# A convolution block and a selective scan on one core: the step is kept in PSUM and multiplied there by VectorE, and per-image work is given one SBUF operand or moved to ScalarE

## What is computed

```python
# layer 0: y = depthwise conv of x with per-image weights agg_w
g  = gelu(conv1x1(y, b1)) * conv1x1(y, b2)
x1 = x + layer_norm_over_channels(g)
# layer 1, on tokens of x1
xh, z = split(x1 @ W_in);  xh = silu(causal_conv_k2(xh))
dt_low, B, C = split(xh @ W_x)
dt = softplus(dt_low @ W_dt + b_dt)                    # the step, 256 channels
h  = exp(dt * A) * h + (dt * xh) * B                   # scan over pixels, 16 states a channel
y  = (sum over states of h * C + xh * D) * silu(z)
m  = y @ W_out
out = silu(group_norm(m) * gamma + beta) + x1          # statistics over a whole image
```

## Time and profile before

| what | value |
|---|---|
| median of 3 runs | 15738.19 us (15737.39 to 15739.81) |
| the profiled execution's own time | 15743.65 us |
| its span | 15741.8 us |
| mean granted TensorE clock | 0.816 of full |
| busy share of the span: POOL, DVE, PE, ACT | 91%, 89%, 73%, 63% |
| share of the DMA queue of the kernel's transfers | 51.9% |

### The profile page before, as it was taken

The page is one execution under the profiler, slowest core; times in us unless marked ns, Lnnn a source line. Parts: engine busy times, 40 slices in busy tenths (PEclk is TensorE's granted clock), DMA queues, the critical chain, the costliest instruction groups (busy, mean ns, idle before and its releaser), DMA issues.

```text
span 15741.8 us, 147189 instructions
## 1 busy us (share of the span) xinstructions
PE 11460.2 (73%) x32388; PEld 3366.9 (21%) x32388; DVE 14038.0 (89%) x11204; ACT 9875.8 (63%) x15964; POOL 14373.3 (91%) x3332
## 2 busy tenths in 40 slices
PE   2777777777777777777777777777777777777777
PEld 1222222222222222222222222222222222222221
DVE  1999999999999999999999999999999999999998
ACT  5666666666666666666666666666666666666666
POOL 1999999999999999999999999999999999999999
PEclk9888788888888888888887888888888878888887
DMA  5555545555555555455555555455555555555554
GB/s 208 122 128 123 127 119 127 125 125 127 122 127 124 129 122 127 119 127 123 127 125 125 123 125 131 120 126 121 129 122 129 125 125 123 123 130 122 125 122 114
DMA packets 1035848, 1990.51 MB, mean 126 GB/s; under 512 B 120065, under 2 KB 121146, under 8 KB 1030714
## 3 DMA queue, kind: packets, MB, share of 16 engines
q1 hardware_dynamic: 1034810, 1979.41, 51.9%
HBM read 1626.62 MB, written 352.32 MB: 126 GB/s over the span
## 4 chain that ended last, share of the span: by engine, by line
POOL 34%; issue 29%; DVE 11%; PE 9%; DMA 8%; ACT 7%; SPq 2%; DVEq 0%; POOLq 0%; ACTq 0%
POOL hq L908 23%; POOL dbx L900 10%; DVE hq L781 5%; DMA dtx_d<-sp 3%; DMA dtx_rep<-dtx_d 3%; PE pp L332 2%; ACT ps_a L574 1%; PE ps_acc L422 1%; PE pp L375 1%; DVE gmv L797 1%; DVE dbx L768 1%; PE pp L381 1%; DVE gmv L806 1%; PE pp L389 1%; SPq L255 1%
## 5 line engine op out<-in xcount | busy, mean ns | idle before, releaser
L908 POOL TENSOR_TENSOR hq<-hq,c_rep 128x2048 f32<-128x2048 f32 x2048 | 9242.7, 4536 | 947.1 <-ACT carry L580 947.1
L781 DVE TENSOR_TENSOR_SCAN hq<-ps_a,carry,dbx 128x512 f32<-128x512 f32 x7168 | 8679.5, 1265 | 573.3 <-POOL dbx L900 329.7
L574 ACT ACTIVATE ps_a<-dt_rep,A_neg 128x512 f32<-128x512 f32 x8192 | 5575.4, 687 | 4916.4 <-DVE hq L781 4902.2
L900 POOL TENSOR_TENSOR dbx<-dtx_rep,b_rep 128x2048 f32<-128x2048 f32 x1024 | 4638.7, 4530 | 24.2 <-DMA dtx_rep<-dtx_d 24.2
L422 PE MATMUL ps_acc<-hq,dsum 128*32 128x512 f32 x16384 | 2480.5, 681 | 1219.8 <-POOL hq L908 1219.6
L768 DVE TENSOR_TENSOR dbx<-dtx_rep,ps_b 128x2048 f32<-128x2048 f32 x1024 | 2316.6, 2262 | 32.3 <-DMA dtx_rep<-dtx_d 30.9
L332 PE MATMUL pp<-xin,diag 128*128 128x504 f32 (+3 forms) x4608 | 2282.7, 614 | 12.8 <-DMA xin<-in_x 12.8
L410 PE MATMUL ps_b<-dbl,bsel 41*128 41x512 f32 x2048 | 1427.4, 783 | 294.7 <-DVE dbx L768 294.6
L366 PE MATMUL pp<-x,W_taps 128*128 128x512 f32 x768 | 690.2, 997 | 1065.1 <-DVE x L744 1065.1
L781 DVE TENSOR_TENSOR_SCAN hq<-ps_a,dbx 128x512 f32<-128x512 f32 x1024 | 1189.1, 1206 | 71.9 <-POOL dbx L900 55.0
L332 PEld LDWEIGHTS pp<-xin,diag 128*128 128x128 f32 x4608 | 772.7, 189 | 1535.5 <-issue 1522.6
(11 more groups left out here) (116 smaller groups left out, 10566.1 us busy)
## 6 DMA issues: line engine op xcount, KB each, us to landing
dt_rep<-dt_d SPq DMA_DIRECT2D x2048, 256.0 KB, 4.5
dtx_rep<-dtx_d SPq DMA_DIRECT2D x2048, 256.0 KB, 5.9
c_rep<-bc_d SPq DMA_DIRECT2D x1024, 256.0 KB, 5.5
b_rep<-bc_d SPq DMA_DIRECT2D x1024, 128.0 KB, 2.9
dt_d<-dt SPq DMA_DIRECT2D x256, 512.0 KB, 2.8
dtx_d<-sp SPq DMA_DIRECT2D x256, 512.0 KB, 5.9
out<-o SPq DMA_DIRECT2D x128, 512.0 KB, 3.5
xin<-in_x SPq DMA_DIRECT2D x192, 320.0 KB, 8.5
```

Of the source, the lines that this page charges most:

```text
L574: A(ps_a[:, i % RA, :], dt_rep[:, q // NQ, g, :], ACT.Exp, scale=A_neg[:, q // NQ, q % NQ, g:g + 1]).then_inc(exp_done, 1)
L781: v.tensor_tensor_scan(hq[:, q % HQ, g, :], ps_a[:, i % RA, :], dbx[:, slot(q), g, :], carry[:, q, g:g + 1] if c % CH else 0.0, ALU.mult, ...
L900: g.tensor_tensor(dbx[:, slot(q), :, :], dtx_rep[:, d, :, :], b_rep[:, c % 2, q % NQ // 2, :].unsqueeze(1).to_broadcast([P, DG, T]), ALU.m ...
L908: g.tensor_tensor(quad, quad, c_rep[:, c % 2, q % NQ, :].unsqueeze(1).to_broadcast([P, DG, T]), ALU.mult).then_inc(cmul_done, 1)
```

## The change

1. `softplus` on DVE writes the step back into PSUM (`pp[:, 0:2]`) and not to `dt`; a new `dt_x` on DVE multiplies it there by `xh` into `dtx`. POOL's `dt_x` goes. A new `evac_dt` on ACT copies the step from PSUM to `dt`, behind the product.
2. The slots of `x_dbl`, of the step's matmul, of the softplus and of the convolution move up by one or two; SP spreads `dtx` ahead of `dt`.
3. `make_diag` moves to ACT as 9 instructions of 128 columns, in the same chunk and slot.
4. Moments and scale: the second moment is read from PSUM, the mean is kept negated, and products by a column are `tensor_scalar`. No DVE instruction there reads two tensors in SBUF any more, and one instruction less is left.
5. SiLU goes in 8 pieces of 512 columns from `o` into the PSUM banks `pp[:, 0]` and `pp[:, 1]` by turns, each waiting for the residual sum two pieces back; DVE adds PSUM and `x1`. It starts one slot later, and all eight sums stand in slot 31.
6. The copy of `x1n` into `x1` moves to ACT, in slot 0 of chunk 1 behind the third `x1` of the image (`keep_first`); PE's product of chunk 2 waits for it.

```diff
-PE_XH, PE_Z, PE_DBL, PE_DT, PE_OUT = (1, 2), (3, 5), 8, 12, 18
-PE_CONV = (8, 9, 10, 11, 13, 14, 15, 16, 17)
+PE_XH, PE_Z, PE_DBL, PE_DT, PE_OUT = (1, 2), (3, 5), 7, 10, 18
+PE_CONV = (8, 9, 11, 12, 13, 14, 15, 16, 17)
-ACT_XZ, ACT_DBL, ACT_SP, ACT_OUT = 5, 10, (13, 14, 15), 23
+ACT_XZ, ACT_DBL, ACT_SP, ACT_DT, ACT_OUT = 5, 9, (12, 13, 14), 17, 23
-DVE_NORM, DVE_Y1, DVE_DT, DVE_Y0, DVE_GATE = 0, 8, 17, 24, 25
-POOL_DTX = 4
-GN_STATS, GN_SUM, GN_MOM, GN_RSTD, GN_SCALE, GN_SILU, GN_ADD = 24, 25, 26, 27, 28, 29, (30, 31)
+DVE_NORM, DVE_Y1, DVE_DT, DVE_Y0, DVE_GATE = 0, 8, 16, 24, 25
+GN_STATS, GN_SUM, GN_MOM, GN_RSTD, GN_SCALE, GN_SILU, GN_ADD = 24, 25, 26, 27, 28, 30, 31
...
+                    spread_dtx(b, c + 1, 0)
                     spread_dt(b, c + 1, 0)
-                    spread_dtx(b, c + 1, 0)
+                    spread_dtx(b, c + 1, 1)
                     spread_dt(b, c + 1, 1)
-                    spread_dtx(b, c + 1, 1)
...
                     pe.wait_ge(x1_done, b * CH + c + 1)
+                    if c == 2:
+                        pe.wait_ge(kept, b + 1)
...
             def group_silu(b):
-                act.wait_ge(gsc_done, 3 * b + 3)
-                for k in range(4):
-                    piece = o[:, k * (L // 4):(k + 1) * (L // 4)]
-                    A(piece, piece, ACT.Silu, scale=gmv[:, 4:5], bias=gmv[:, 5:6]).then_inc(silu_done, 1)
+                act.wait_ge(gsc_done, 2 * b + 2)
+                for k in range(CH):
+                    if k >= 2:
+                        act.wait_ge(fin_done, CH * b + k - 1)
+                    A(pp[:, k % 2, :], o[:, k * T:(k + 1) * T], ACT.Silu, scale=gmv[:, 4:5],
+                      bias=gmv[:, 5:6]).then_inc(silu_done, 1)
...
+            def evac_dt(b, c):
+                act.wait_ge(dtx_done, b * CH + c + 1)
+                if not (isinstance(b, int) and b * CH + c == 0):
+                    act.wait_ge(dt_out, 16 * (b * CH + c))
+                A(dt[:], pp[:, 0:2, :], ACT.Copy).then_inc(dt_done, 1)
+
+            def make_diag(b):
+                for k in range(TAPS):
+                    last = A(diag[:, k, :], w["ident"][:], ACT.Identity,
+                             scale=wts[:, bass.ds(b, 1), k:k + 1].rearrange("p o k -> p (o k)"))
+                last.then_inc(diag_ready, 1)
+
+            def keep_first(b):
+                act.wait_ge(x1_done, b * CH + 3)
+                A(x1[:, 1:1 + 2 * T], x1n[:, 1:1 + 2 * T], ACT.Copy).then_inc(kept, 1)
...
-                v.scalar_tensor_tensor(dt[:], pp[:, 0:2, :], 0.0, sp[:], ALU.max, ALU.add).then_inc(dt_done, 1)
+                v.scalar_tensor_tensor(pp[:, 0:2, :], pp[:, 0:2, :], 0.0, sp[:], ALU.max, ALU.add).then_inc(step_done, 1)
+
+            def dt_x(b, c):
+                dve.wait_ge(step_done, b * CH + c + 1)
+                v.tensor_tensor(dtx[:], pp[:, 0:2, :], xh[:, c % 2, :, :], ALU.mult).then_inc(dtx_done, 1)
...
-                v.tensor_copy(gmv[:, 0:2], pp[:, 1, 0:2]).then_inc(gmv_done, 1)
+                v.tensor_scalar(gmv[:, 0:1], pp[:, 1, 0:1], -1.0, None, ALU.mult).then_inc(gmv_done, 1)
                 dve.wait_ge(gmv_done, 3 * b + 1)
-                v.scalar_tensor_tensor(gmv[:, 2:3], gmv[:, 0:1], gmv[:, 0:1], gmv[:, 1:2], ALU.mult,
+                v.scalar_tensor_tensor(gmv[:, 2:3], gmv[:, 0:1], gmv[:, 0:1], pp[:, 1, 1:2], ALU.mult,
...
-                v.tensor_tensor(gmv[:, 4:5], gmv[:, 3:4], w["gn"][:, 0:1], ALU.mult).then_inc(gsc_done, 1)
-                dve.wait_ge(gsc_done, 3 * b + 1)
-                v.tensor_tensor(gmv[:, 5:6], gmv[:, 0:1], gmv[:, 4:5], ALU.mult).then_inc(gsc_done, 1)
-                dve.wait_ge(gsc_done, 3 * b + 2)
-                v.tensor_tensor(gmv[:, 5:6], w["gn"][:, 1:2], gmv[:, 5:6], ALU.subtract).then_inc(gsc_done, 1)
+                v.tensor_scalar(gmv[:, 4:5], gmv[:, 3:4], w["gn"][:, 0:1], None, ALU.mult).then_inc(gsc_done, 1)
+                dve.wait_ge(gsc_done, 2 * b + 1)
+                v.tensor_scalar(gmv[:, 5:6], gmv[:, 0:1], gmv[:, 4:5], w["gn"][:, 1:2], ALU.mult, ALU.add).then_inc(gsc_done, 1)
...
-                v.tensor_tensor(o[:, s], o[:, s], x1[:, 1 + s.start:1 + s.stop], ALU.add).then_inc(fin_done, 1)
+                v.tensor_tensor(o[:, s], pp[:, k % 2, :], x1[:, 1 + s.start:1 + s.stop], ALU.add).then_inc(fin_done, 1)
```

More of the change, by code:

```diff
@@ L864, in _ @@
             softplus(0, 0)
+            dt_x(0, 0)
             gate(0, 1)
```

54 lines of the change are left out of this document (19 added, 35 removed).

## The result

The changed kernel takes **14764.67 us** (median of 4 runs, 14764.23 to 14765.01), the kernel before 15737.79 beside it (4 runs, 15735.61 to 15739.81). The ratio is 0.9382, with a 95% interval of 0.9365 to 0.9398. Predicted were 14,765. The total fits; whether each term does is another question, and some of them do not.

A forecast was written before the change was run, and what follows sets the result against it. POOL was taken to bound regular chunks, with DVE's two-SBUF-operand instructions waiting for it in chunks 6 and 8. -31.0 us an image times 31 is -961; with -6 and -10, 14,767, less 5, rounded to 14,765; range 14,640 to 15,010.

The forecast's parts named there:

- POOL's chunk of 53.8: Regular chunks: POOL loses the product of the step, so its chunk goes from 56.1 to 53.8 us.
- The product, 1.25, and DVE's chunk of 54.5: Regular chunks: DVE's product costs 1.25 us, a 0.29 wait goes; DVE's chunk is 54.5 us and becomes the bound.
- Rival D: Regular chunks: POOL stays the bound, 53.8 us in place of 54.5, total 14,610; chance 0.66 together with the forecast.
- ACT's copy at no cost: Regular chunks: ACT's new copy of the step, 1.02 us, was taken to cost DVE's path 0.
- Rival B: Every chunk: the step's copy puts ACT and PE onto DVE's path, 0.8 us a chunk, +200, total 14,965; chance 0.20.
- Diagonals: Chunk 6: nine ACT instructions of 0.3 us, 0.2 on the path; the chunk becomes 54.7 us, -11.8.
- Moments and scale, -5.7 and -8.7: Chunk 8: line 797 falls from 5.91 to about 0.25 us; lines 806 and 808 become one instruction of 0.2.
- rival A: Chunk 8: one-source variance and second scale lines still wait for POOL, 5.7 and 4.3 us, total 15,075; chance 0.11.
- SiLU, sums, copy, +0.3: Chunk 8: a wait of 3.0 us, one more scan covering 1.1, and 5.9 for the pieces: 8.9 against 8.6.
- the term for waits on POOL: Chunk 8: DVE's waits on POOL fall away, put at -1.0 us.
- Chunk 1, +1.3: Chunk 1: ACT's copy delays xh, mostly behind a table load, +0.4; with +1.25 and -0.3 this makes +1.3 us.
- The sum: Whole image: the chunks' terms sum to -32.0 us, -31.0 against the mean image of 481.5; times 31 is -961.

The follow-up runs named there:

- gate swap: Slots of DVE's output gate and layer-0 gate swapped (25 and 24 instead of 24 and 25), against the changed kernel: 14499.47 us, ratio 0.9214.

## Why the prediction was right, step by step

*What bounded the kernel*: right. While POOL works, DVE with two SBUF operands waits or makes POOL wait, and DVE with one in PSUM does not: 254 of the changed kernel's 256 products run wholly within instructions of POOL, without one exception.

*POOL's chunk of 53.8*: right, 53.82 where it is the bound.

*The product, 1.25, and DVE's chunk of 54.5*: 1.25 and 54.43. The 0.29 of the softplus went, as expected. Rival D's side is excluded by 0.5 us of POOL's idle time a chunk, and by the gate swap.

*ACT's copy at no cost*: right where it was to decide. DVE's waits ahead of line 788 sum up to 235.6 us over the run, 236.9 before. PE now waits 0.6 us for the copy in a chunk, and that is taken up behind it. Rival B is out.

*Diagonals*: chunk 6 at 54.43 in place of 54.7. The nine take 0.386 each and not 0.3, but nothing of them lies on the path, where 0.2 was put.

*Moments and scale, -5.7 and -8.7*: right; rival A is out at one column. The run with two columns shows what the variance line would have cost if it had waited: 1.26 us in chunk 8, where the rival had 5.7, and 30 us over the run, where it had 177. Its price was a stall of the kernel before, which does not carry over.

*SiLU, sums, copy, +0.3*: **this step failed in size.** The wait ahead of the sums was to be 3.0 and is 4.12. The error is in "one more scan covers it". Timeline of ACT in the changed kernel:

```profile
7139.16 0.69 ACT L575 ACTIVATE ps_a<-dt_rep,A_neg 128x512 f32<-128x512 f32 x1 [0.42 <-DVE hq L811]
...
7141.13 1.28 ACT L594 ACT_TABLE_LOAD   x1
7142.43 2.32 ACT L594 ACTIVATE pp<-o,gmv 128x512 f32<-128x512 f32 x3
```

ACT's table load for SiLU stands behind a decay (line 575) that itself waits for a scan of DVE. A slot later is later for both, so the scan covers nothing; 1.1 us too few. The part costs 53 us in the changed kernel, where I had +0.3 and, for the copy in chunk 1, +0.4, together 0.7 x 31 = 22. In chunk 8 itself the sums part costs 1.5 us (4.12 and 6.02, 8.6 before) and not 0.3. What made good for it is the term for waits on POOL: put at 1.0, it was 1.8, two waits of 0.70 and 1.08 in chunk 8 of the kernel before that are gone. So 68.73 against 68.5 is two errors that largely cancel.

*Chunk 1, +1.3*: 55.26 against 53.6 is +1.7, and **the path of this term was wrong too**. The copy was to delay `xh`, mostly behind a table load. It does not: ACT forms `xh` 10.65 us behind the chunk's first scan with the copy on ACT, and 10.65 without it. What waits for the copy is PE, 1.1 us at its first product of the chunk, and how much of that reaches DVE hangs on TensorE's clock. Timeline of PE in chunk 1, in the changed kernel and then in the run with the diagonals back on DVE as one instruction, which keeps the copy:

```profile
7156.48 2.08 PE L367 MATMUL pp<-x,W_taps 128*128 128x512 f32 x2 [17.14 <-ACT x L612]
...
7160.05 1.91 PE L367 MATMUL pp<-x,W_taps 128*128 128x512 f32 x2
```

```profile
1299.81 2.07 PE L367 MATMUL pp<-x,W_taps 128*128 128x512 f32 x2 [17.67 <-ACT x L606]
...
1303.21 1.02 PE L367 MATMUL pp<-x,W_taps 128*128 128x512 f32 x2
```

Both times PE comes from over 17 us of idle time and starts at the lower level of the clock (granted 0.50, 1.06 us a matmul). In the changed kernel the higher level comes 9.7 us behind the chunk's first scan, in the other image 7.1. With the late rise the matmuls of `z` end late, so ACT waits 0.62 for them:

```profile
7165.15 0.60 ACT L559 ACTIVATE sz<-pp 128x512 f32<-128x512 f32 x1 [0.62 <-PE pp L390]
```

Its next table load and decays come late in turn, and DVE's scan waits 0.82 for a decay. Leaving out the first image, the rise comes 8.9 to 9.8 us behind the first scan in 30 of the changed kernel's images, and their chunk 1 takes 54.0 to 54.4 us; in the one with a rise at 8.3 it takes 53.6. In the other run a rise by 7.5 gives 53.5 in 20 images, a later one 54.3 to 54.7 in 11, with the same copy. Without the copy, in the run with sums and copy as before, PE starts 1.1 us sooner, and chunk 1 takes 53.5 with a rise as late as 9.0. So the 0.82 that this run gives back in chunk 1 takes both, the copy and a late rise of the clock. Why the rise comes when it does stays open.

*The sum*: an image takes 450.57 us (from the norm of chunk 8 at 6634.51 to 7085.08), 481.5 - 31.0 = 450.5 were predicted. The fit to a microsecond is luck: the sum gave 14,762 before it was rounded to 14,765, and +0.2 in chunk 8 and +0.4 in chunk 1 stand against -0.3 in chunk 6 and -0.07 in each of the five others of 54.43.

*What the prediction did not see*: the parts do not add up. Alone on the kernel before, the diagonals bring 278 and the product part 580; undone from the changed kernel, they cost 128 and 326. I had priced each from the stalls of before, which is right for the whole change made at once, and for none of its parts alone. This is also why three of my expectations for single parts missed (the diagonals on DVE, moments and scale, the product with two SBUF operands): all priced a stall by those of the kernel before.

## What to carry to other kernels

An instruction of DVE that lasts many times its peers' length waits inside itself: look at where POOL's instruction of that moment ends. Give such an instruction one operand in PSUM, or a single source and one column, or another engine; but its price depends on POOL's backlog, so measure it in the kernel in which it will stand, and do not add up prices taken singly. When an operand or a piece is moved to avoid such a wait, see first whether POOL works at that moment: the sums here gained 53 us on two SBUF operands in one order of the work and lost 69 in another, in part because another step had come ahead of them in their slot. A rate of a secondary engine is no floor for a stretch in which it may fall behind and catch up later.

## What was unexpected of the hardware

- The exclusion between DVE and POOL stretches POOL too: 10.36 and 10.13 us for two instructions of 4.5 when DVE gets in first.
- With POOL in arrears DVE lost twice running (8.50 us for 1.35 of work, though it asked 2.8 us ahead of POOL's next instruction); with DVE as the bound it lost once at most in the diagonals, twice in 8 of 256 products with both operands in SBUF, and ties within 20 ns went either way. The two kernels with such ties (the diagonals on DVE, the product part alone) spread by 76 and 95 us from run to run, the changed kernel by 1.
- A one-source instruction of DVE waits with 128 columns (4.60 us once in nine) and with 2 (1.41), and never with 1 (0.153).
- TensorE's granted clock in a regular chunk rose from 0.83 to 0.87 of its higher level (0.816 to 0.858 over the run), with the same 126 matmul records in it. It did not decide the regular chunk; in chunk 1, where PE starts at the lower level, the moment of its rise decides over 0.8 us an image.
